# An attention and mixture-of-experts block on one core: second maxima ahead of queries and keys, probabilities between two groups of copies

## The reference

```python
x = x + attention(layernorm(x), Wq, Wk, Wv, Wo)      # 16 heads of 8, each token sees itself and the 63 before it
x = x + experts(layernorm(x), w_router, w1, w2, bias) # 8 experts, top 2, capacity 2048 tokens an expert
```

## Time and profile before

| what | value |
|---|---|
| median of three runs | 877.89 us |
| profiled execution, its own time | 880.53 us |
| its span, first to last instruction | 878.8 us |
| attention, first to last shift (L1142) | 17.88 to 538.04 us |
| busy in the span: TensorE matmul | 747.0 us (85%) |
| VectorE | 518.8 us (59%) |
| ScalarE | 452.3 us (51%) |
| GpSimd | 356.4 us (41%) |
| granted TensorE clock, mean over the span | 0.934 |
| the same from 279.47 to 345.68 us (batch 4) | 1.00 |

### The profile page before, as it was taken

One profiled execution on the slowest core, in us unless ns is written; L12 is line 12 of the kernel. 1 busy time (PEld: TensorE's weight loads), 2 busy tenths in 40 slices (PEclk: granted clock), 3 DMA queues, 4 the chain that ended last, 5 costly groups with the idle time before them and its releaser, 6 DMA issues.

```text
span 878.8 us, 19093 instructions
## 1 busy us (share of the span) xinstructions
PE 747.0 (85%) x7425; PEld 540.9 (62%) x7425; DVE 518.8 (59%) x1592; ACT 452.3 (51%) x923; POOL 356.4 (41%) x318
## 2 busy tenths in 40 slices
PE   6999999999999999999999997205997988988970
PEld 3566666566566566566566664205997887887870
DVE  6887878978878888878878878401221211221110
ACT  5576685675676576576585563103452333333320
POOL 3000000024123123123123253660777777777877
PEclk9999999999999999999999998557999899999995
DMA  5941000001100101100100111113354544554533
GB/s 138 389 151 55 7 15 7 33 29 33 43 30 30 47 29 31 46 29 29 46 30 30 49 46 53 55 41 105 33 105 60 106 82 60 105 84 58 85 31 33
DMA packets 50130, 54.20 MB, mean 62 GB/s; under 512 B 6017, under 2 KB 39448, under 8 KB 49024
## 3 DMA queue, kind: packets, MB, share of 16 engines
q0 software_dynamic: 22528, 17.22, 13.5%
q1 hardware_dynamic: 27520, 35.86, 12.2%
HBM read 17.70 MB, written 31.59 MB: 56 GB/s over the span
## 4 chain that ended last, share of the span: by engine, by line
PE 36%; DVE 24%; issue 16%; POOL 15%; DMA 6%; another core or an unknown queue 1%; SPq 1%; POOLq 1%; ACT 0%; DVEq 0%; ACTq 0%
POOL out L444 14%; PE u_ps L1150 6%; PE sT_ps L1125 5%; DVE kmax L688 5%; PE sT_ps L1142 4%; DVE moving L702 3%; DMA out<-y_sb,xg 3%; PE o_ps L1159 3%; DVE negmax L694 2%; PE tail_ps L1165 2%; DVE negmax_hl L699 2%; PE tail_ps L1170 2%; PE o_ps L1134 2%; DMA x_sb<-in_L_attn_x 2%; DVE ctx_sb L714 2%
## 5 line engine op out<-in xcount | busy, mean ns | idle before, releaser
L444 POOL DMA_INDIRECT out<-y_sb,xg x128 | 198.8, 1553 | 81.5 <-DVE y_sb L1059 42.0
L363 POOL DMA_INDIRECT slots_dram<-send_rows,slot_id x112 | 110.1, 983 | 178.9 <-PE sT_ps L1142 134.5
L521 ACT ACTIVATE probsT<-sT_ps 128x1024 f32<-128x1024 f32 x128 | 132.1, 1032 | 62.4 <-PE sT_ps L1142 57.3
L688 DVE TRANSPOSE_TENSOR_REDUCE kmax<-sT_ps 128x32 f32<-128x1024 f32 x128 | 159.4, 1245 | 7.6 <-PE sT_ps L1125 7.1
L620 ACT ACTIVATE hT<-sT_ps 128x512 f32<-128x512 f32 x128 | 76.6, 598 | 143.9 <-PE sT_ps L1354 114.2
L1125 PE MATMUL sT_ps<-qbd,kT 64*128 64x256 f32 x1024 | 133.2, 380 | 0.0
L378 POOL TENSOR_TENSOR xbias<-x_sb,bias_sb 128x256 f32<-128x256 f32 x32 | 23.4, 732 | 246.3 <-PE sT_ps L1142 246.3
L1354 PE MATMUL sT_ps<-xT_hl,w_hl 128*128 128x512 f32 x384 | 103.8, 423 | 18.3 <-DVE xT_hl L1046 18.3
L1125 PEld LDWEIGHTS sT_ps<-qbd,kT 64*128 64x128 f32 x1024 | 98.5, 191 | 9.8
L1354 PEld LDWEIGHTS sT_ps<-xT_hl,w_hl 128*128 128x128 f32 x384 | 75.0, 202 | 35.2 <-issue 13.1
L1046 DVE TENSOR_TENSOR xT_hl<-u_ps,xT_hl 128x512 fp32r<-128x512 f32 x32 | 22.1, 690 | 109.0 <-ACT xT_hl L613 105.9
(11 more groups left out here) (171 smaller groups left out, 1130.0 us busy)
## 6 DMA issues: line engine op xcount, KB each, us to landing
slots_dram<-empty_rows SPq DMA_DIRECT2D x8, 1096.0 KB, 16.5
xg<-slots_dram SPq DMA_DIRECT2D x32, 274.0 KB, 3.5
out<-xbias SPq DMA_DIRECT2D x32, 128.0 KB
w_sb<-in_L_ffn_w SPq DMA_DIRECT2D x16, 256.0 KB
send_rows<-rows_sb SPq DMA_DIRECT2D x7, 548.0 KB, 3.2
out<-y_sb,xg POOLq DMA_INDIRECT x128
slots_dram<-send_rows,slot_id POOLq DMA_INDIRECT x112
out<-empty_rows SPq DMA_DIRECT2D x1, 1024.0 KB, 24.8
```

The costliest lines, as they stand in the source:

```text
L363: pool.indirect_dma_start(out=slots_dram, out_offset=bass.IndirectOffsetOnAxis(ap=slots[:, k, j:j + 1].bitcast(U32), axis=0), in_=rows[:, ...
L444: pool.indirect_dma_start(out=out, out_offset=bass.IndirectOffsetOnAxis(ap=xg[:, r, 4 * c + k, ROW - 1:ROW].bitcast(U32), axis=0), in_=y_s ...
L521: nc.scalar.activation(probsT[:, gp].rearrange("p b k h q -> p (b k h q)"), sT_ps[:, gp].rearrange("p b c -> p (b c)"), ACT.Exp).then_inc( ...
L688: nc.vector.tensor_reduce(kmax[:, u % 2, :], sT_ps[:, u % 2].rearrange("p b (c q) -> p (b c) q", q=32), AX.X, ALU.max, apply_transpose=Tru ...
```

## The change

On TensorE the maxima of the odd unit move ahead of the queries and keys (odd slots) and of the transposes (even slots), right behind the output projection of the slot. On ScalarE `query_key` is split: the four copies of the queries stay where they were, the two of the keys, with the count `s_k_sb`, come behind the second unit's probabilities. Before the first slot the two parts follow each other as they did. No instruction is added or removed, and TensorE's wait for `s_k_sb` in front of the values is as before.

```diff
@@ ScalarE @@
-            def query_key(n, p, bank=proj_ps):
+            def queries(n, p, bank=proj_ps):
                 act.wait_ge(s_qk, n + 1)
...
+            def keys(n, p, bank=proj_ps):
                 for gp in range(2):
                     last = nc.scalar.activation(kT[:, gp, BLK + p * 2 * P:BLK + (p + 1) * 2 * P],
                                                 bank[:, 2 * P:4 * P], ACT.Copy, scale=evenodd[:, gp:gp + 1])
...
                 if t % 2 == 1 and (t < 5 or not last):
-                    query_key(b * PAIRS + (t + 3) // 2, (t + 3) // 2 % PAIRS)
+                    queries(b * PAIRS + (t + 3) // 2, (t + 3) // 2 % PAIRS)
...
                 exps(g, 1)
+                if t % 2 == 1 and (t < 5 or not last):
+                    keys(b * PAIRS + (t + 3) // 2, (t + 3) // 2 % PAIRS)
@@ TensorE @@
                     project(g - 2)
+
+                if t == 5 and not first:
+                    pe.wait_ge(s_xn2T_sb, 2 * (b - 1) + 1)
+                maxima_T(2 * g + 1)
                 if t % 2 == 1 and (t < 5 or not last):
                     query_key(b * PAIRS + (t + 3) // 2, (t + 3) // 2 % PAIRS)
...
-                if t == 5 and not first:
-                    pe.wait_ge(s_xn2T_sb, 2 * (b - 1) + 1)
-                maxima_T(2 * g + 1)
                 pe.wait_ge(s_exp, 2 * g + 1)
```

More of the change, by code:

```diff
@@ L586, in _ @@
             act.wait_ge(c_dve, 1)
-            query_key(0, 0)
+            queries(0, 0)
+            keys(0, 0)
             act.wait_ge(c_dve, 2)
@@ L592, in _ @@
             normed_T(1, 1, u_ps)
-            query_key(1, 1, u_ps)
+            queries(1, 1, u_ps)
+            keys(1, 1, u_ps)
             normed(2)
```

## The result

The changed kernel takes 889.8 us (median of four runs, 888.9 to 890.47) against 877.84 us for the kernel before in the same runs: ratio 1.0135, 95% interval 1.0118 to 1.0153, 12.0 us slower. I had said 882.3 us, 877.5 to 889.0. The direction is right, the size is off by a factor of 2.7.

A forecast was written before the change was run, and what follows sets the result against it. TensorE, the fullest engine in the attention phase, was taken as the bound, with 23.3 us of waits for VectorE's `moving`. Terms -8.3 + 13.5 - 0.8 = +4.4 us on 877.89 gave 882.3 us, range 877.5 to 889.0 (8 in 10).

The forecast's parts named there:

- The stall at the values: Odd slots: TensorE waits for the keys' copies before the values, 24 times 0.42 us and six times 0.57, 13.5 us lost.
- slot 1's gain: Slot 1's first half: 0.8 us gained in batches 0 to 2, 3.2 in batches 3 to 7 by avoiding GpSimd's issue.
- price (b): TensorE's new order is longer, through the way into the 32-column maxima: about 0.09 us more a slot.
- the time given back: Slots 2 and 4: TensorE's standing time lets VectorE finish `moving` earlier, so `kmax` starts sooner: 0.8 us gained.
- First halves: From one slot's first shift to its second: early maxima gain 8.3 us in all, lower bound 2.8.
- Slots 3 and 7: First halves: slot 3 gains 1.2 us over 7 batches; slot 7 gains 2.3 in batches 2 to 6 as its cast runs freely.
- Slots 0 and 4: First halves: slot 0 gains 0.2 us in all, slot 4 gains 0.5 over three batches, taken as 0.4.
- the bound of 0.10: Upper limit, in us a slot, on how much longer TensorE's new order gets; the lower limit was 0.
- S': The start of the second unit's shift in a slot, where the slot's second half begins.
- The collisions stay: Rival: slots 1 and 7 keep their waits tied to GpSimd's DMAs, +9.9 us, 887.8 us; chance 0.25.
- Every wait goes: Rival: all TensorE waits before second units' shifts vanish, VectorE's small steps included; 5 us gained, 872.9 us; chance 0.10.
- The wait at the values: Rival: this wait is hidden if ScalarE finishes by 1.84 us after the second shift; chance within the 0.13 and 0.10.

The follow-up runs named there:

- experiment 6: The changed kernel run again unmodified for its trace, on one chip with the unchanged kernel: 887.08 us, ratio 1.0111 to the kernel before.
- experiment 2: Kernel before with only ScalarE's order changed, the keys' copies behind the second unit's probabilities: 887.05 us, ratio 1.0146.
- experiment 5: The kernel before run again unmodified for its trace: 872.17 us, ratio 0.9983 to itself.
- 3: Changed kernel with slot 5 of batches 1 to 7 put back as before on both engines: 881.07 us, ratio 1.0079 to the kernel before.
- experiment 11: Changed kernel without GpSimd's two sends in slot 0's second half, each later pair one half further on: one run, 882.31 us.
- 1: Kernel before with only TensorE's order changed, the second unit's maxima right behind the projected output: 872.3 us, ratio 0.9997.
- 4: Kernel before with GpSimd's two sends moved from slot 1's first half to its second: 872.56 us, ratio 0.9982.
- 9: Kernel before with the second unit's maxima moved ahead in slots 3, 4 and 7 only, ScalarE unchanged: 870.54 us, ratio 0.9969.
- 10: Kernel before with the second unit's maxima moved ahead in slots 1, 3, 4 and 7, ScalarE unchanged: 871.13 us, ratio 0.9976.
- 7: Changed kernel with TensorE's values behind the second fill instead of ahead of it: 878.11 us, ratio 1.005 to the kernel before.
- experiment 8: Changed kernel with two 512-column matmuls of zeros behind the router's in slot 6: 885.37 us, ratio 1.0144 to the kernel before.

## Why the prediction was right or wrong

The stall, which makes the loss, came as forecast. What failed are the other terms of the sum, and all of them towards too small a loss: slot 1's gain, price (b), the time given back, and the clock, for which the sum had nothing.

**The stall at the values, 13.5 us: right.** Measured 14.0 us (experiment 6) and 13.0 by itself (experiment 2). 24 stalls of 0.44 instead of 0.42, six of 0.56 instead of 0.57, 30 waits as counted. It passed on whole, as said; the next shift waited for nothing.

**First halves, 8.3 us gained: 7.0 measured.** Slots 3 and 7 came as worked out, 1.2 and 2.5 us (1.2 and 2.3 to 2.5 predicted), the latter because the cast starts 0.31 into GpSimd's issue and is still free there. Slot 1 is the step that failed: I gave its batches 3 to 7 3.2 us, but where `negmax` is on time they go from 4.26 to 4.05, 1.0 us (experiments 5 and 6), and where it was late it stayed so with the maxima early (the profile after, four of five). Slots 0 and 4 gained more than I had given them, 1.5 and 1.0 us.

**Price (b), 0.09 us a slot: mis-sized, it is 0.19 in odd slots up to the fill's last eight matmuls.** The order costs 0.08 on the way into the maxima, as read, and 0.11 more on the way out, between queries and keys (0.54, before 0.43): the bound of 0.10 was too low. In slots 1, 3 and 7 this did not show, since the fill is followed by the shift 0.86 after its matmuls' start and not 0.96: both use 64 rows. In slot 5, where other transposes follow the fill, it did: 4.50 instead of 4.31, 1.1 us lost instead of 0.5. The Trainium skill, "TensorEngine Tiling (Array Packing)", Key Properties, has TensorE drained when the tiling mode changes, and not when only the tile does; 0.96 and 0.86 agree with it.

**"In slots 2 and 4 ... 0.8 us" given back, and slot 0: wrong in sign.** I had VectorE's lead as a gain. Second halves of slots 0, 2 and 4 became 2.5, 0.6 and 0.1 us longer. In slot 0 VectorE takes 0.15 more from the shift on, since S' comes earlier and its small steps do not, and this moved the cast from 2.83 to 2.98 after S', 0.51 into GpSimd's issue, where it takes 0.47 us: 0.15 and 0.29 in five batches. Before, it started 0.35 into that issue and was free. I had looked for collisions that go and not for one that comes. With slot 0's first half this is 1.0 us lost where I had 0.2 gained. In the changed kernel's first profile this collision is absent: the cast starts at 2.98 there too, but GpSimd's second send only at 2.88 to 2.91, and the half takes 3.97. So the collision does not bear on that profile, and what made the sends late in it is open.

**The clock: a term that was not in the sum at all.** Two slots 6 at half clock cost 3.8 us in experiment 6; four instead of one made slot 6 longer by 5.4 in the profile after. I had read the clock as 1.00 for batch 4 only, and had not asked of batch 6, whose slot 6 took 5.45 us instead of 4.46. Slots 6 at half clock, of seven in each profile: the kernels whose values wait for the keys had 4, 3, 3, 2 and 0 (after, experiments 2, 3, 6, 11), 12 of 35; those without that wait and with the usual router 1, 0, 1, 0, 1, 1 and 1 (before, 1, 4, 5, 9, 10, 7), 5 of 49.

These counts look as if the stalls brought the fall, but they do not show it. Read from the clock rows, the changes in one profile, in the attention and behind it, all lie on one even raster of times, to within 3 ns, and this raster stands differently against the kernel in each profile. Carried on through the whole profile, one of its points comes 1.62 to 2.29 us after the shift of slot 6 in 18 of the 91 slots. In 17 of them the clock falls, at such a point; the 18th is batch 5 of experiment 8, with the two added matmuls. In the other 73 the nearest points are at 1.54 or less and at 2.32 or more, and none of them is slow. So where the slot happens to stand against the raster decides in the single case. The stalls move the slots against it, as anything does that changes the length of a batch, and the number of slow slots in one profile is chance: 3.8 and 5.4 us are not a fixed price of the change. A forecast could have given this term a range, and not a value.

The terms, in us: stall 13.5 became 14.0; first halves -8.3 became -7.0; given back by the halves behind them -0.8 became +3.2; clock 0 became +3.8 (slot 6 as a whole). Together 4.4 became 14.0 in the attention. The two profiles of the first comparison, with their late `negmax` and `kmax`, give by the same count 14.5, -6.8, +1.4 and +5.4, together 14.5. That is 2.0 more than the 12.0 of the medians of the first comparison and 1.3 more than the 12.7 between experiment 6's median and that of the kernel before beside it; the spread of what lies behind the attention is larger than either.

**The rivals.** "The collisions stay" came nearest in total (+9.9), by luck: slot 7's collision went, and slot 1's had never been. "Every wait goes" fell: 11.2 of 23.3 us of waits stay. The wait at the values was not hidden.

## What to carry to other kernels

- Before moving a copy behind another piece of work, look for who waits for that copy's count because of the bank and not because of the data: the values did not need the keys, they needed their place.
- A gain in one half of a loop is worth only what the next half does not take back. Moving the maxima only in slots 3, 4 and 7, where nothing behind them took the gain back, shortened the attention by 2.7 us (0.3% of the whole); moving them in all slots gave no measurable difference.
- A lateness that repeats in five batches of one trace can still belong to that execution or its chip. A second trace of the same kernel is the cheapest experiment; here it would have taken 2.2 us out of the sum.

## What the runs showed of the hardware

- VectorE's cast is held up by GpSimd's indirect issue only in a late part of it: casts that start 0.03 to 0.49 us after the start of line 363 take 0.18 us, those from 0.51 to 0.52 take 0.47, those at 0.59 (experiment 11) 0.39, at 0.75 (experiment 5) 0.23, and from 0.82 on 0.18, but for single places with 0.25 to 0.33. The casts that start from 0.51 to 0.75 all end 0.98 to 0.99 after the issue's start. A shift of 0.15 us decides between none and 0.29.
- The granted clock fell to 0.50 (1.2 GHz) in single slots, each time at or behind the second of the router's two groups of 8-column matmuls, while TensorE's busy time in the stretch before was full (1.74 of 1.74 us): the busy share does not show it, the clock column does. It fell at 17 of the 18 places where the raster of that profile's clock changes met this part of the slot, and nowhere else.
- A group of 64-row matmuls follows another 0.10 us sooner than one in another tiling mode (0.86 and 0.96 us after the start of the fill's last eight).
